# Sine of a sum in the feed-forward layer: compares and corrections replaced by two sines and column factors

## Chip, cores and metric

The kernel runs on all 8 cores of one Trainium2 chip, each core on its own batch row, without communication. The metric is the device time of the slowest core in microseconds. In the profile PE is TensorE, DVE is VectorE, ACT is ScalarE, POOL is GpSimd and SP is SyncE.

## What is computed

Two transformer layers of different make on x of shape (8, 2048, 1024): attention and a feed-forward layer, then attention and a mixture of experts, each with a residual sum and a layer norm. The change touches the first feed-forward layer:

```python
def _quantum_transform(hidden, theta, w_real, w_imag):
    imag = w_imag * jnp.sin(theta + hidden * 0.1)
    quantum_phase = jnp.cos(theta) * w_real + jnp.sin(theta) * w_imag
    return hidden + quantum_phase * imag * 0.1
hidden = jnp.einsum('bsd,df->bsf', x, W1) + b1          # 1024 -> 4096
q = _quantum_transform(hidden, quantum_phases, quantum_weights_real, quantum_weights_imag)
act = jax.nn.relu(q)
return jnp.einsum('bsf,fd->bsd', act, W2) + b2           # 4096 -> 1024
```

theta, w_real and w_imag have one value per hidden feature (4096 of them); theta is a normal value times 2 pi, so it can be well outside of -pi to pi.

## The kernel before

The activations lie transposed: a feature on each of 128 partitions, tokens along the free axis, in 8 blocks of 128 features, X in f32 and a copy XB in bf16. The 2048 tokens are cut into 4 pieces (tq) of TQ = 512.

Everything is written out by hand. The helpers vop (VectorE), aop (ScalarE) and mm (TensorE) add an instruction to their engine's program with an increment of that engine's counter (sV, sA, sT). vop and aop put a wait on the engine's own counter ahead of each instruction, so each waits until its predecessor has ended. Other waits come from the waits argument; Prog.wait leaves out one whose value the engine has already waited for. In the profile all DVE instructions stand at L323, all ACT instructions at L332, matmuls at L305 (L301 with an increment), DMA issues at L277; they are told apart by their tiles.

Prologue: constants and small vectors are loaded on SP's queue, the vectors transposed on TensorE and put into the columns of COLS. sin(theta) and cos(theta) are made once in the scratch tile PSCR (columns 320:352 and 352:384) by sin32, which reduces the argument on DVE first. COLS holds, for the feed-forward layer, theta reduced to -pi to pi (columns 32:64), ecol = 0.1 w_imag (cos(theta) w_real + sin(theta) w_imag) in 72:104 and b1 in 104:136.

ffn0 (from line 1194) treats the tokens in two halves of two pieces each. In a half, the first product runs over 8 slabs of W1 (fs), each with 4 blocks of 128 hidden features (fsub), each for both pieces (ti): 64 tiles of 128x512. A tile is 8 matmuls into one of four PSUM buffers that rotate, and then, over buffers that alternate between two places (par):

- ACT: B1 = 0.1 psum + theta (Identity, bias a column), B0 = psum (Copy), which frees the PSUM buffer
- DVE: B4 = (B1 >= pi), B1 = B1 - 2 pi B4, B4 = (B1 < -pi), B1 = B1 + 2 pi B4
- ACT: SINB = Sin(B1)
- DVE: B2 = ecol SINB + B0
- ACT: HID = Relu(B2 + b1) in bf16

The program of each engine holds the tiles one behind the other, in just this order. The second product follows in the same half: 8 blocks of output features, each for two pieces, 32 matmuls each over HID; DVE adds the result and the bias column b2 to X. W1 and W2 are loaded by POOL's queue in pieces of 1 MB into two slots of WBf, each load waiting for the last matmul that used its slot. A layer norm follows (post_ln_scoped), then attention and the experts.

Of the kernel before, what the change touches and what calls it, by code (L numbers as in the profile page):

```python
# [7 lines left out]
F32 = mybir.dt.float32  # L8
BF16 = mybir.dt.bfloat16
I32 = mybir.dt.int32  # L10
AX = mybir.AxisListType.X
AF = mybir.ActivationFunctionType
ALU = mybir.AluOpType
# [5 lines left out]
TQ = 512  # L19
# [3 lines left out]
TWO_PI = 2.0 * math.pi  # L23
# [167 lines left out]
def build_program(phases=(0, 1, 2, 3)):  # L191
# [13 lines left out]
    def sb(name, shp, dt=BF16, st=None):  # L205
        t = (st or top).enter_context(nc.sbuf_tensor(name, shp, dt))
        wb_birth[id(t)] = sT.n if "sT" in locals() or True else 0
        return t

    with top:  # L210
# [14 lines left out]
        SMALLF = sb("SMALLF", [128, 512], F32)  # L225
        COLS = sb("COLS", [128, 160], F32)
        QCOL = sb("QCOL", [128, 24], F32)
# [4 lines left out]
        CONER = sb("CONER", [1, 128], F32)  # L232
        CE64AB = sb("CE64AB", [96, 128], F32)
        CSEL128 = sb("CSEL128", [128, NC * NH], BF16)
# [12 lines left out]
        RI32A = sb("RI32A", [128, TQ], I32)  # L247
        CEPS = sb("CEPS", [128, 1], F32)

        PS = [top.enter_context(nc.psum_tensor(f"ps{i}", [128, 512], F32))  # L250
# [8 lines left out]
        def bs(pst, sem, val):  # L259
            psum_owner[id(pst)] = (sem, val)  # L260
# [56 lines left out]
        def vop(name, *args, waits=(), **kw):  # L317
            P.em("vector", lambda E, v=sV.n: E.wait_ge(sV.h, v))
            for (sem, val) in waits:
                P.wait("vector", sem, val)  # L320
            v = sV.inc()
            P.em("vector", lambda E, nm=name, a=args, k=kw:
                 getattr(E, nm)(*a, **k).then_inc(sV.h, 1))  # L323
            return v
# [47 lines left out]

        vop("memset", CEPS[:, :], EPS)
        v_x = dma("sync", "x", X[:, :].rearrange("p (c t) -> p c t", c=NC), dx.rearrange("(c p) t -> p c t", p=128))
        v_consts = 0
        for (name, tile) in (("c_ones", CONES), ("c_eye_f32", CEYEF),
                             ("c_eye_bf", CEYEB),
                             ("c_ones_row_f32", CONER), ("c_e64ab", CE64AB),
                             ("c_qsel", CSEL128),
                             ("c_tri", CTRI), ("c_iotak", CIOTAK),  # L380
                             ):
            v_consts = dma("sync", "consts", tile[0:tile.shape[0], :], dram[name])
# [4 lines left out]
        with contextlib.ExitStack() as pre:  # L387
# [70 lines left out]
            vop("tensor_scalar", COLS[:, 72:104], PSCR[:, 384:416], 0.1, None, ALU.mult)  # L458
            v_thb = v_thst

# [733 lines left out]
        def ffn0(v_in_v, a_in_a, atc_in=None):  # L1194
# [6 lines left out]
            with st:  # L1201
# [4 lines left out]
                B2 = sb("B2f", [128, 2 * TQ], F32, st)  # L1206
                B4 = sb("B4f", [128, 2 * TQ], BF16, st)
                SINB = sb("SINB", [128, 2 * TQ], F32, st)
# [7 lines left out]
                for half in range(2):  # L1216
# [3 lines left out]
                    for fs in range(8):  # L1220
# [3 lines left out]
                        for fsub in range(4):  # L1224
                            fc = fs * 4 + fsub
                            thb = COLS[:, 32 + fc:33 + fc]
                            ecol = COLS[:, 72 + fc:73 + fc]
                            b1c = COLS[:, 104 + fc:105 + fc]
                            for ti, tq in enumerate(tqs):
# [3 lines left out]
                                for c in range(NC):  # L1233
# [10 lines left out]
                                qsl = slice(par * TQ, (par + 1) * TQ)  # L1244
                                a_t = aop("activation", B1[:, qsl], pa[:, :],
                                          AF.Identity, scale=0.1, bias=thb,
                                          waits=((sT, vt), (sV, v_thb)))
                                a_t = aop("activation", B0[:, qsl], pa[:, :],
                                          AF.Copy, waits=())
                                bs(pa, sA, a_t)  # L1250
                                vop("tensor_scalar", B4[:, qsl], B1[:, qsl],
                                    math.pi, None, ALU.is_ge, waits=((sA, a_t),))
                                vop("scalar_tensor_tensor", B1[:, qsl], B4[:, qsl],
                                    -TWO_PI, B1[:, qsl], ALU.mult, ALU.add)
                                vop("tensor_scalar", B4[:, qsl], B1[:, qsl],
                                    -math.pi, None, ALU.is_lt)
                                vv = vop("scalar_tensor_tensor", B1[:, qsl],
                                         B4[:, qsl], TWO_PI, B1[:, qsl], ALU.mult,
                                         ALU.add)
                                a_sin = aop("activation", SINB[:, qsl], B1[:, qsl],  # L1260
                                            AF.Sin, waits=((sV, vv),))
                                vv = vop("scalar_tensor_tensor", B2[:, qsl],
                                         SINB[:, qsl], ecol, B0[:, qsl], ALU.mult,
                                         ALU.add,
                                         waits=((sA, a_sin),
                                                (sA, use_f.get(("rl", par), 0))))
                                dst = HID[:, fc * 1024 + ti * TQ:
# [330 lines left out]
```

## Time and profile before

| | |
|---|---|
| time, median of 2 runs | 7404.08 us (7343.23 and 7464.92) |
| profiled execution | 7338.63 us; span of its slowest core 7337.1 us |
| spans of the 8 cores | 7309.3 to 7337.1 us |
| PE busy | 4699.5 us, 64% |
| DVE busy | 2767.2 us, 38% |
| ACT busy | 2083.1 us, 28% |
| POOL busy | 170.7 us, 2% |
| DMA | 160.88 MB, mean 22 GB/s |

The profile is of one execution, on its slowest core. The span goes from the first to the last instruction; the execution's time has 1.5 us more around it. The granted clock is the share of full speed that TensorE's clock was given, as a mean over a stretch. Busy shares are means over stages of very different make; the feed-forward layer lies between 2012 and 3068 us of the span.

### The profile page before, as it was taken

To read this page: it belongs to the slowest core of one execution; us is meant where nothing else is said; L and a number is where in the kernel's file an instruction comes from. 1 tells how busy PE (TensorE), PEld (TensorE's weight loads), DVE (VectorE), ACT (ScalarE), POOL (GpSimd) and SP (SyncE) were. 2 spreads that over 40 slices of the span, in tenths; PEclk is the share of its full clock that TensorE was granted. 3 is DMA by queue.
4 is the path that set the end of the run, shared out by engine and by line. 5 is a ranking of instruction groups with operands and counts; after the bars stand their busy time and mean duration, and the time that the engine had idled before them with its cause. 6 is when DMAs were issued, how large, how long until landed. Compare 5 with 4: busy or idle time off the path is not lost.

```text
span 7337.1 us, 65020 instructions; the slowest of 8 cores (7309.3 to 7337.1 us)
## 1 busy us (share of the span) xinstructions
PE 4699.5 (64%) x17489; PEld 1732.6 (24%) x17489; DVE 2767.2 (38%) x4355; ACT 2083.1 (28%) x3175; POOL 170.7 (2%) x186
## 2 busy tenths in 40 slices
PE   1455777873255755735444667773599999998772
PEld 0221222221011311301111122221244444443230
DVE  2524422215544344346434333235433333332114
ACT  2233344533333133222122455633111111111012
POOL 0000000000000000000000000000000000000000
PEclk8777888986566866855657788886799999999885
DMA  1111000000011411400001110000222222222321
GB/s 50 24 18 12 4 9 9 1 12 0 12 18 23 52 23 18 41 12 12 0 0 15 12 12 9 1 12 0 35 35 35 35 35 35 35 35 38 55 46 46
DMA packets 236271, 160.88 MB, mean 22 GB/s; under 512 B 138921, under 2 KB 225494, under 8 KB 233878
## 3 DMA queue, kind: packets, MB, share of 16 engines
q0 software_dynamic: 232320, 138.92, 14.2%
q1 hardware_dynamic: 3606, 17.79, 0.7%
q8 instruction: 164, 2.69, 0.2%
q14 instruction: 181, 1.48, 0.1%
HBM read 287.21 MB, written 8.39 MB: 40 GB/s over the span
## 4 chain that ended last, share of the span: by engine, by line
PE 52%; DVE 25%; ACT 11%; issue 6%; DMA 5%; DVEq 1%; SPq 0%; ACTq 0%; POOL 0%; POOLq 0%
PE ps L305 36%; PE ps L301 15%; DVE SMALLF L323 6%; ACT SQR L332 3%; DVE B1f L323 2%; DVE FQR L323 2%; DVE B4f L323 2%; DVE SCpa L323 1%; DVE B2f L323 1%; DMA WBq<-w_qkv 1%; ACT HID L332 1%; ACT B1f L332 1%; DMA WBm<-ws_u 1%; DVE X L323 1%; ACT SINB L332 1%
## 5 line engine op out<-in xcount | busy, mean ns | idle before, releaser
L305 PE MATMUL ps<-XB,WBm 128*128 128x512 bf16 x4480 | 1118.5, 391 | 67.2 <-DMA WBm<-ws_g 56.3
L305 PE MATMUL ps<-PT,ARV 128*64 128x512 bf16 (+2 forms) x1152 | 485.4, 421 | 392.6 <-DVE XB L323 268.6
L305 PE MATMUL ps<-XB,WBf 128*128 128x512 bf16 x896 | 371.1, 585 | 436.5 <-ACT B0f L332 376.9
L332 ACT ACTIVATE SGR<-ps 128x512 bf16<-128x512 f32 x320 | 191.0, 597 | 1585.1 <-PE ps L301 893.2
L305 PEld LDWEIGHTS ps<-XB,WBm 128*128 128x128 bf16 x4480 | 446.3, 100 | 636.4 <-issue 139.3
L305 PE MATMUL ps<-HPAIR,WBm 128*128 128x512 bf16 x2272 | 545.7, 383 | 60.4 <-DMA WBm<-ws_d 60.4
L332 ACT ACTIVATE PT<-ps,BIASC 128x512 bf16<-128x512 f32 (+3 forms) x640 | 398.7, 623 | 492.8 <-PE ps L301 356.0
L323 DVE TENSOR_TENSOR ps<-ps,CTRI 128x128 f32<-128x128 f32 x512 | 153.5, 300 | 1015.9 <-PE ps L301 988.3
L332 ACT ACTIVATE PT<-ps,BIA 128x512 bf16<-128x512 f32 (+3 forms) x640 | 398.7, 623 | 396.8 <-PE ps L301 232.8
L301 PE MATMUL ps<-PT,CONES 128*128 128x512 bf16 (+3 forms) x1280 | 496.4, 388 | 0.0
L323 DVE RECIPROCAL SMALLF<-ps 64x512 f32<-64x512 f32 x128 | 429.4, 3355 | 66.7 <-PE ps L301 51.0
L305 PE MATMUL ps<-XB,WBkv 128*128 128x512 bf16 x960 | 323.4, 496 | 161.4 <-ACT ARK L332 86.4
L301 PE MATMUL ps<-SQR,CONES 128*128 128x512 bf16 x192 | 108.7, 566 | 409.8 <-ACT SQR L332 409.8
L323 DVE SCALAR_TENSOR_TENSOR USR<-ps,WBC 128x512 f32<-128x512 f32 x256 | 177.1, 692 | 514.4 <-PE ps L301 514.4
L323 DVE SCALAR_TENSOR_TENSOR X<-ps,X 128x512 f32<-128x512 f32 x288 | 199.2, 692 | 404.1 <-PE ps L301 402.3
L305 PEld LDWEIGHTS ps<-PT,ARV 128*64 128x64 bf16 x1152 | 126.5, 110 | 810.0 <-issue 802.5
L305 PEld LDWEIGHTS ps<-HPAIR,WBm 128*128 128x128 bf16 x2272 | 224.0, 99 | 335.8 <-issue 73.5
L305 PEld LDWEIGHTS ps<-XB,WBf 128*128 128x128 bf16 x896 | 107.6, 129 | 693.3 <-issue 677.1
L301 PE MATMUL ps<-AUXR,NEGE 128*128 128x512 bf16 x640 | 257.6, 402 | 7.5 <-DVE AUXR L323 7.5
L305 PE MATMUL ps<-ARQ,ARK 128*128 128x512 bf16 x640 | 260.9, 408 | 0.0
L301 PE MATMUL ps<-XB,WBm 128*128 128x512 bf16 x640 | 246.9, 386 | 0.0
L323 DVE TENSOR_SCALAR B4f<-B1f 128x512 bf16<-128x512 f32 x256 | 109.3, 427 | 344.6 <-ACT B0f L332 331.0
(225 smaller groups left out, 5161.7 us busy)
## 6 DMA issues: line engine op xcount, KB each, us to landing
WBf<-w_ff POOLq DMA_DIRECT2D x32, 1024.0 KB, 11.5
WBq<-w_qkv POOLq DMA_DIRECT2D x64, 256.0 KB, 4.4
WBm<-we_g POOLq DMA_DIRECT2D x16, 1024.0 KB, 11.0
WBm<-we_u POOLq DMA_DIRECT2D x16, 1024.0 KB, 15.0
WBm<-we_d POOLq DMA_DIRECT2D x16, 1024.0 KB, 11.5
X<-x SPq DMA_DIRECT2D x1, 8192.0 KB, 38.1
WBkv<-w_qkv POOLq DMA_DIRECT2D x8, 1024.0 KB, 9.2
WBm<-ws_g POOLq DMA_DIRECT2D x8, 1024.0 KB, 8.8
```

What stands on the lines that cost most here:

```text
L301: E.matmul(o, l, r, start=a, stop=b, tile_position=t)
L305: E.matmul(o, l, r, start=a, stop=b, tile_position=t))
L323: getattr(E, nm)(*a, **k).then_inc(sV.h, 1))
L332: getattr(E, nm)(*a, **k).then_inc(sA.h, 1))
```

## The change

In each tile of the first product the argument of the sine is no longer made and reduced. By sin(theta + z) = cos(theta) sin(z) + sin(theta) cos(z), with z = 0.1 psum, ACT makes B1 = Sin(z + pi/2), SINB = Sin(z) and B0 = psum, all three from PSUM and one behind the other; the third frees the PSUM buffer. DVE then makes B1 = sin(theta) B1, B1 = cos(theta) SINB + B1, and B2 = ecol B1 + B0. Relu is as before. The two compares, the two corrections and the buffer B4 go.

The prologue puts sin(theta) and cos(theta) into COLS (160:192 and 192:224) with two copies, COLS grows from 160 to 224 columns, CPI2 holds pi/2, and the constant c_e64ab, which nothing reads, is no longer loaded. The first Sin of a tile gets a wait for the B2 of the tile that used its buffers before.

```diff
--- before.py
+++ after.py
@@ -223,14 +223,13 @@
         XB = sb("XB", [128, NC * T], BF16)
         SQR = sb("SQR", [128, 2 * TQ], BF16)
         SMALLF = sb("SMALLF", [128, 512], F32)
-        COLS = sb("COLS", [128, 160], F32)
+        COLS = sb("COLS", [128, 224], F32)
         QCOL = sb("QCOL", [128, 24], F32)
         KVC = sb("KVC", [128, 8], F32)
         CONES = sb("CONES", [128, 128], BF16)
         CEYEF = sb("CEYEF", [128, 128], F32)
         CEYEB = sb("CEYEB", [128, 128], BF16)
         CONER = sb("CONER", [1, 128], F32)
-        CE64AB = sb("CE64AB", [96, 128], F32)
         CSEL128 = sb("CSEL128", [128, NC * NH], BF16)
         CTRI = sb("CTRI", [128, 128], F32)
         CIOTAK = sb("CIOTAK", [128, 16], F32)
@@ -246,6 +245,7 @@
         GSCRB = sb("GSCRB", [128, NC * 16], BF16)
         RI32A = sb("RI32A", [128, TQ], I32)
         CEPS = sb("CEPS", [128, 1], F32)
+        CPI2 = sb("CPI2", [128, 1], F32)
 
         PS = [top.enter_context(nc.psum_tensor(f"ps{i}", [128, 512], F32))
               for i in range(6)]
@@ -371,11 +371,12 @@
             slot_use[key] = max(slot_use.get(key, 0), vt)
 
         vop("memset", CEPS[:, :], EPS)
+        vop("memset", CPI2[:, :], math.pi / 2.0)
         v_x = dma("sync", "x", X[:, :].rearrange("p (c t) -> p c t", c=NC), dx.rearrange("(c p) t -> p c t", p=128))
         v_consts = 0
         for (name, tile) in (("c_ones", CONES), ("c_eye_f32", CEYEF),
                              ("c_eye_bf", CEYEB),
-                             ("c_ones_row_f32", CONER), ("c_e64ab", CE64AB),
+                             ("c_ones_row_f32", CONER),
                              ("c_qsel", CSEL128),
                              ("c_tri", CTRI), ("c_iotak", CIOTAK),
                              ):
@@ -456,7 +457,9 @@
             vop("tensor_tensor", PSCR[:, 384:416], PSCR[:, 384:416], PSCR[:, 32:64],
                 ALU.mult)
             vop("tensor_scalar", COLS[:, 72:104], PSCR[:, 384:416], 0.1, None, ALU.mult)
-            v_thb = v_thst
+            vop("tensor_copy", COLS[:, 160:192], PSCR[:, 320:352],
+                waits=((sA, va2),))
+            v_thb = vop("tensor_copy", COLS[:, 192:224], PSCR[:, 352:384])
 
             vl = dma("sync", "cols", SMALLF[0:1, 0:NH], dram["slopes"],
                      waits=((sV, sV.n), (sT, sT.n), (sA, sA.n)))
@@ -1204,7 +1207,6 @@
                 B0 = sb("B0f", [128, 2 * TQ], F32, st)
                 B1 = sb("B1f", [128, 2 * TQ], F32, st)
                 B2 = sb("B2f", [128, 2 * TQ], F32, st)
-                B4 = sb("B4f", [128, 2 * TQ], BF16, st)
                 SINB = sb("SINB", [128, 2 * TQ], F32, st)
                 w1 = dram["w_ff1"].rearrange("(c p) n -> p c n", p=128)
                 w2 = dram["w_ff2"].rearrange("(f p) n -> p f n", p=128)
@@ -1223,7 +1225,8 @@
                                      WSLOT)
                         for fsub in range(4):
                             fc = fs * 4 + fsub
-                            thb = COLS[:, 32 + fc:33 + fc]
+                            sthc = COLS[:, 160 + fc:161 + fc]
+                            cthc = COLS[:, 192 + fc:193 + fc]
                             ecol = COLS[:, 72 + fc:73 + fc]
                             b1c = COLS[:, 104 + fc:105 + fc]
                             for ti, tq in enumerate(tqs):
@@ -1242,28 +1245,26 @@
                                 wuse(WBf, slot, vt)
                                 par = (fc * 2 + ti) % 2
                                 qsl = slice(par * TQ, (par + 1) * TQ)
-                                a_t = aop("activation", B1[:, qsl], pa[:, :],
-                                          AF.Identity, scale=0.1, bias=thb,
-                                          waits=((sT, vt), (sV, v_thb)))
-                                a_t = aop("activation", B0[:, qsl], pa[:, :],
+                                a_cz = aop("activation", B1[:, qsl], pa[:, :],
+                                           AF.Sin, scale=0.1, bias=CPI2[:, 0:1],
+                                           waits=((sT, vt),
+                                                  (sV, use_f.get(("b1", par), 0))))
+                                aop("activation", SINB[:, qsl], pa[:, :],
+                                    AF.Sin, scale=0.1, waits=())
+                                a_h = aop("activation", B0[:, qsl], pa[:, :],
                                           AF.Copy, waits=())
-                                bs(pa, sA, a_t)
-                                vop("tensor_scalar", B4[:, qsl], B1[:, qsl],
-                                    math.pi, None, ALU.is_ge, waits=((sA, a_t),))
-                                vop("scalar_tensor_tensor", B1[:, qsl], B4[:, qsl],
-                                    -TWO_PI, B1[:, qsl], ALU.mult, ALU.add)
-                                vop("tensor_scalar", B4[:, qsl], B1[:, qsl],
-                                    -math.pi, None, ALU.is_lt)
-                                vv = vop("scalar_tensor_tensor", B1[:, qsl],
-                                         B4[:, qsl], TWO_PI, B1[:, qsl], ALU.mult,
-                                         ALU.add)
-                                a_sin = aop("activation", SINB[:, qsl], B1[:, qsl],
-                                            AF.Sin, waits=((sV, vv),))
+                                bs(pa, sA, a_h)
+                                vop("tensor_scalar", B1[:, qsl], B1[:, qsl],
+                                    sthc, None, ALU.mult,
+                                    waits=((sA, a_h), (sV, v_thb)))
+                                vop("scalar_tensor_tensor", B1[:, qsl],
+                                    SINB[:, qsl], cthc, B1[:, qsl], ALU.mult,
+                                    ALU.add)
                                 vv = vop("scalar_tensor_tensor", B2[:, qsl],
-                                         SINB[:, qsl], ecol, B0[:, qsl], ALU.mult,
+                                         B1[:, qsl], ecol, B0[:, qsl], ALU.mult,
                                          ALU.add,
-                                         waits=((sA, a_sin),
-                                                (sA, use_f.get(("rl", par), 0))))
+                                         waits=((sA, use_f.get(("rl", par), 0)),))
+                                use_f[("b1", par)] = vv
                                 dst = HID[:, fc * 1024 + ti * TQ:
                                           fc * 1024 + (ti + 1) * TQ]
                                 a_hid = aop("activation", dst, B2[:, qsl], AF.Relu,
```

## Rows read from the trace of the kernel before

**Rows 1.** Cores: span in us, mean granted clock.
```profile
core 0: 7309.3 us, clock 0.786
core 2: 7337.1 us, clock 0.782
```

**Rows 2.** Stretches, first half's products: length, busy (x instructions) of PE, PEld, DVE, ACT, POOL, clock, DMA.
```profile
2012.00:2439.00 427.00, 225.02 (x563) 69.36 (x564) 191.69 (x321) 169.49 (x257) 8.59 (x8) 0.63 0.16 22
2439.00:2540.00 101.00, 101.00 (x470) 45.78 (x469) 25.01 (x32) 0.38 (x1) 11.61 (x8) 1.00 0.72 73
```

**Rows 3.** Chain of waits in 2000 to 2240 us, shares by engine and line.
```profile
by line: DVE B1f L323 19.9%; DVE B4f L323 12.4%; DVE B2f L323 10.5%; ACT HID L332 10.0%; ACT B1f L332 9.8%; issue 9.8%; ACT SINB L332 9.0%; ACT B0f L332 8.6%; DMA WBf<-w_ff 5.8%; PE ps L305 1.3%; DVEq L318 0.9%; ACTq L61 0.7%; DVEq L61 0.6%
```

**Rows 4.** Timeline, ACT: start us, length us, instruction, [idle before <- released by].
```profile
2201.11 0.72 ACT L332 ACTIVATE HID<-B2f,COLS 128x512 bf16<-128x512 f32 x1 [0.96 <-DVE B2f L323]
2201.97 0.69 ACT L332 ACTIVATE B1f<-ps,COLS 128x512 f32<-128x512 f32 x1
2202.75 0.60 ACT L332 ACTIVATE B0f<-ps 128x512 f32<-128x512 f32 x1
2206.10 0.63 ACT L332 ACTIVATE SINB<-B1f 128x512 f32<-128x512 f32 x1 [2.75 <-DVE B1f L323]
2207.69 0.72 ACT L332 ACTIVATE HID<-B2f,COLS 128x512 bf16<-128x512 f32 x1 [0.96 <-DVE B2f L323]
```

**Rows 5.** Timeline, DVE, the same tile.
```profile
2203.45 0.43 DVE L323 TENSOR_SCALAR B4f<-B1f 128x512 bf16<-128x512 f32 x1 [2.44 <-ACT B0f L332]
2203.98 0.69 DVE L323 SCALAR_TENSOR_TENSOR B1f<-B4f,B1f 128x512 f32<-128x512 bf16 x1
2204.78 0.43 DVE L323 TENSOR_SCALAR B4f<-B1f 128x512 bf16<-128x512 f32 x1
2205.31 0.69 DVE L323 SCALAR_TENSOR_TENSOR B1f<-B4f,B1f 128x512 f32<-128x512 bf16 x1
2206.84 0.75 DVE L323 SCALAR_TENSOR_TENSOR B2f<-SINB,COLS,B0f 128x512 f32<-128x512 f32 x1 [0.83 <-ACT SINB L332]
```

**Rows 6.** Timeline, PE, a tile at the low clock (its 8 matmuls in two rows).
```profile
2210.07 3.14 PE L305 MATMUL ps<-XB,WBf 128*128 128x512 bf16 x7 [3.89 <-ACT B0f L332]
2213.01 0.63 PE L301 MATMUL ps<-XB,WBf 128*128 128x512 bf16 x1
```

**Rows 7.** Groups of ACT by form: count, busy us, mean ns; the last: the layer alone.
```profile
L332 ACT ACTIVATE PT<-ps,BIASC 128x512 bf16<-128x512 f32 x448 | 307.8, 687 | 397.9 <-PE ps L301 293.0 <-DVE ps L323 68.3 <-ACT PT L332 5.7
L332 ACT ACTIVATE SGR<-ps 128x512 bf16<-128x512 f32 x320 | 191.0, 597 | 1585.1 <-PE ps L301 893.2 <-DVE HPAIR L323 691.9
L332 ACT ACT_TABLE_LOAD x1 | 1.3, 1283 | 2.7 <-DVE B1f L323 2.7
```

**Rows 8.** Tile X in 2432 to 2560 us: ns min/median/max of the bias add.
```profile
L323 DVE TENSOR_SCALAR X<-X,COLS x16: 486/578/1644, 2439.6 to 2539.8; 128x512 f32<-128x512 f32 x16
```

**Rows 9.** Waits of PE in 2432 to 2545 us: total, times, longest.
```profile
PE ps L301 <- ACT HID L332: 8.9, 1, 8.9
```

**Rows 10.** Waits in 2013 to 2432 us, POOL's loads and PE's on loads.
```profile
POOL WBf L277 <- PE ps L301: 405.4, 8, 52.8
PE ps L305 <- DMA WBf<-w_ff: 59.6, 1, 59.6
```

**Rows 11.** Timeline of the prologue, SP's issues and PE's first matmul.
```profile
10.25 2.42 SPq L277 DMA_DIRECT2D CE64AB<-c_e64ab  x1
42.37 0.24 PE L314 MATMUL ps<-CEYEF,SMALLF 8*128 8x8 f32 x1 [42.37 <-DMA SMALLF<-ln_g]
```

**Rows 12.** Timeline, POOL's issues of loads and a DVE instruction beside one.
```profile
2412.68 1.67 POOL L277 DMA_DIRECT2D WBf<-w_ff  x1 [51.72 <-PE ps L301]
2442.65 1.67 POOL L277 DMA_DIRECT2D WBf<-w_ff  x1 [28.30 <-PE ps L301]
2443.06 1.49 DVE L323 TENSOR_SCALAR X<-X,COLS 128x512 f32<-128x512 f32 x1 [0.17 <-DVE X L323]
```

**Rows 13.** Timeline, DVE, bias add with no load beside it.
```profile
2439.61 0.49 DVE L323 TENSOR_SCALAR X<-X,COLS 128x512 f32<-128x512 f32 x1 [0.18 <-DVE X L323]
```

## The prediction, made before the change was run

> **What bounds the kernel now.** I read the cores first: all eight do the same work, each on its own batch row, and the slowest, core 2, has a span of 7337.1 us [rows 1]. No engine is full over the whole run, so the edited stage has to be read alone. The busy times by stretch do that [rows 2]: the first product of the feed-forward layer's first half takes some 425 us, in which PE is busy for 225 us, DVE for 192 and ACT for 169, at a granted clock of 0.63. Nobody is full. The second product of 101 us is PE at full clock from end to end. (The second half shows the same two stretches.) The chain of waits inside the first product [rows 3] says why nobody is full: DVE and ACT lines alternate (B1f, B4f, B2f, HID, SINB, B0f) and PE has 1.3%. It is a latency chain across two engines, not a throughput limit.
>
> The timelines of ACT and DVE show it tile by tile [rows 4, 5]. ACT executes in program order, and Relu of a tile (HID) waits for DVE's B2f, so the next tile's first activation stands behind it: tiles don't overlap on ACT and DVE. One period, from HID to HID, is 2201.11 to 2207.69 = 6.58 us, and 2 halves of 32 x 2 tiles make 128 periods, 842 us. PE is not the limit: at its low level (1.2 GHz) a tile runs from 2210.07 to 2213.64, 3.57 us [rows 6]; with the 0.25 us from the end of B0f to a tile's first matmul that is 3.8 us in a period of 6.58.
>
> **The period before, start to start** [rows 4, 5]: HID to B1f 0.86, B1f to B0f 0.78, B0f to the first compare 0.70, then on DVE 0.53, 0.80, 0.53, last B1f to SINB 0.79, SINB to B2f 0.74, B2f to HID 0.85. Sum 6.58, as it must be. It also gives the steps between instructions: about 0.09 us from ACT to ACT (0.15 behind HID), 0.105 from DVE to DVE, 0.10 from one engine to the other.
>
> **The period after.** Four DVE instructions go (two compares of 0.427, two corrections of 0.693). The Identity activation becomes a Sin with a pointer bias, the other Sin moves ahead and reads PSUM, and DVE gets one tensor_scalar and one scalar_tensor_tensor, each with a column pointer. Step by step:
> - HID to the first Sin: 0.86, unchanged. Its new wait is on the B2f of two tiles ago, older than what the Relu before it has waited for, so nothing is issued for it. In the first two tiles there is none.
> - First Sin, PSUM to SBUF, 128x512, bias from a column. The trace has no Sin of that form, but Exp in it takes 687 ns, and B1f 0.69 us [rows 4, 7]. To the next start 0.78.
> - Second Sin, from PSUM without pointer. Silu in that form takes 597 ns [rows 7], the old Sin from SBUF 629. I take 597, for the form decides in every other pair of rows: 0.69 to the next start (bound 0.72).
> - Copy, 597 ns as now, and the step to DVE: 0.70.
> - tensor_scalar, f32 SBUF to SBUF with one column: the form of the bias add X<-X,COLS of the second product, 486 ns undisturbed [rows 8]. With 0.105: 0.59.
> - scalar_tensor_tensor with two f32 inputs and a column: the form of B2f, 0.752 [rows 5]. With 0.105: 0.86.
> - B2f as before, to HID: 0.85. Its wait on an old Relu is again covered by a younger one.
>
> Sum 5.33; with the third decimals kept 5.32. In short: between Copy and B2f, 0.53 + 0.80 + 0.53 + 0.79 + 0.74 = 3.39 us go and 0.69 + 0.59 + 0.86 = 2.14 come. The gain is 1.26 us a tile; a misreading of 0.02 in it would be 2.5 us in all.
>
> **How many tiles count.** The second product starts under the tail of the first. The last matmul of its first group waits 8.89 us for the Relu of the tile before the last [rows 9], and its second group, which ends just before 2442.2, takes longer than the last tile's chain. So 63 of 64 tiles in each half are on the path: 126 x 1.26 = 158.8 us.
>
> **What the other parts cost.** The activation table is loaded once in the whole layer, 1.283 us [rows 7], in the first tile's chain; it moves to the front of that chain and costs the same. PSUM buffers come free after three ACT instructions instead of two, but four rotate and PE needs 3.8 of 5.32 us: nothing; without that cover it would be 0.69 a tile. The weight loads have a slot of eight tiles, 42.6 us; today PE waits for one only at the layer's start, and POOL sits up to 52.8 us before it may issue the next [rows 10]: hidden. In the prologue the SP queue issues one load less (2.42 us), but the first transposition starts at 42.37, when its column lands [rows 11], seven issues and 30 us later: no gain taken (at most 2.42). Two small copies and a memset there cost some 0.3 us each on DVE, two of them on the path: +0.6.
>
> **DVE against the issue of loads.** In the second product X<-X,COLS takes up to 1.644 us instead of 0.486 when POOL issues a weight load beside it: issue at 2442.65 for 1.67, DVE 2443.06 to 2444.55 [rows 8, 12]. The new tensor_scalar has that form, and 8 loads are issued inside each first product [rows 10]. If each met one: 16 x 1.16 = 18.5 us. By the timeline a load follows the start of the tile's last matmul by 1.2 to 1.6 us, at the low clock 4.4 to 4.8 us after the Copy; the next tensor_scalar starts at 5.42. The twelve issues of 0.87 us are about over by then, the four of 1.67 (as at 2412.68) are not. I take 2 us, bounds 0 and 18.5. The Trainium skill, "SBUF — State Buffer", section "SBUF: two separate sides", gives a rule for such rows: a DVE instruction in a two-port mode and a GpSimd one exclude each other for the whole instruction. By that rule the price per meeting is the one that the rows show, and it speaks against this form of instruction, which the first product doesn't have with f32 output today.
>
> **Sum.** The profiled execution took 7338.6 us: 7338.6 - 158.8 + 0.6 + 2 = 7182.4. I predict **7182 us**, 2.1% below it. The profiled execution lies near the lower of the two times shown (7343.2); their median, 7404, is 65 us higher, and a median over runs that spread alike would be 7247.
>
> **Rivals.**
> 1. *The steps inside an engine are wider than read.* X<-X,COLS starts 0.18 us behind the instruction that it depends on, not 0.105 [rows 13]. On the three steps that are new (Sin to Copy, and two on DVE) 0.075 more each would cost 3 x 0.075 x 126 = 28 us: 7210, within 2%. Against it: that row stands behind a second wait in its program, which none of the new ones has, and B1f behind B4f depends on its predecessor too and shows 0.105. Chance 0.13.
> 2. *DVE and POOL meet at every load*: 7338.6 - 158.2 + 18.5 = 7199. Against it stands the timing above. Chance 0.05.
> 3. *The table is reloaded.* If Sin and Copy needed different tables, one load a tile would be 128 x 1.283 = 164 us and take the gain away (7344), and two a tile would give 7508, slower. It decides from one load per tile on. Against it: one load in the layer today, with Sin, Relu, Identity and Copy mixed. Chance 0.02. The Trainium skill, "ScalarE: Activation LUTs", section "Table sets: the hidden batching unit", says that relu, copy and identity are in every set; by that rule no load is added, and the trace agrees with its one load.
> 4. *The gain is given back later.* The granted clock differs by stretch (0.63 and 1.00, [rows 2]), and shifted starts may shift where it falls and rises in the attention and expert stages. Equal cores differ by 28 us in span (7309.3 and 7337.1) [rows 1], so 10 to 20 us either way are possible: up to 7202. Chance 0.10 upward; downward it stays faster.
>
> **How the numbers follow.** The forecast has 0.70. What a measurement of this kernel can tell from no change is about 2%, here 147 us; the sum has 11 us more than that, so the wider steps, the meetings at every load and half of rival 4 end within 2%. Faster 0.76 (the forecast, and half of rival 4), within 2% 0.22, slower 0.02. The range reaches from 7150 (rival 4 downward, with the prologue's 2.42 and the 2 us of meetings saved and some rounding) to 7250 (rivals 1, 2 and 4 together, 7182 + 28 + 17 + 20 = 7247, and the median of runs that spread as before).
>
> **What would show it.** In the changed kernel HID to HID should be 5.32 us; the Sins 687 and 597 ns; the tensor_scalar 486 ns except beside a load; its successor 752; steps on DVE 0.105. The first product of each half should last some 79 us less (348 instead of 427), PE waiting there for B0f still, at a granted clock somewhat above 0.63, with one ACT_TABLE_LOAD in the layer. The second products and the other stages should keep their lengths within some 10 us. I am wrong if a Sin from PSUM takes longer than an Exp, if table loads appear, if PE becomes what ACT waits for, or if the other stages move.

## Result

| | before | changed |
|---|---|---|
| median | 7438.36 us (26 runs) | 7312.73 us (27 runs) |
| lowest | 7339.85 us | 7182.03 us |
| highest | 7662.34 us | 7496.45 us |

In most executions of either kernel some cores have a lower mean granted clock and take up to some hundred us longer, which sets the median; the ratio here and the times named below for single kernels (the lowest of each) leave such runs out. The ratio is 0.9755, with a 95% interval of 0.9707 to 0.9804: the change makes the kernel faster, and whether by more than 2% the interval just leaves open. From lowest to lowest the gain is 158 us, 2.15%. The profile after is that of the changed kernel's execution of 7180.4 us in after_again.

The cores of that execution: span and mean granted clock (they answer to [rows 1]).
```profile
core 0: 7165.9 us, clock 0.799
core 3: 7178.8 us, clock 0.798
```
Its stretches, as in [rows 2]: length, then busy time of PE, PEld, DVE, ACT and POOL with their instructions, granted clock, DMA share, GB/s. The first fence has the four products of the feed-forward layer, the second all that lies before and behind the layer.
```profile
2008.00:2353.00 345.00, 192.11 (x553) 62.13 (x552) 128.31 (x193) 167.93 (x257) 8.60 (x8) 0.74 0.19 25
2353.00:2449.00 96.00, 96.00 (x446) 43.57 (x445) 23.62 (x29) 0.00 (x0) 10.94 (x7) 1.00 0.74 77
2449.00:2798.00 349.00, 195.42 (x576) 64.07 (x575) 129.59 (x195) 166.66 (x256) 9.47 (x9) 0.76 0.20 27
2798.00:2906.00 108.00, 104.24 (x479) 46.73 (x477) 24.63 (x31) 16.84 (x11) 10.05 (x6) 0.99 0.59 59
```
```profile
0.00:2008.00 2008.00, 1129.60 (x4005) 385.10 (x4006) 702.95 (x1077) 734.39 (x1123) 37.02 (x46) 0.78 0.09 14
2906.00:4988.00 2082.00, 1122.38 (x3466) 335.66 (x3466) 855.14 (x1353) 730.87 (x1106) 39.57 (x46) 0.71 0.07 8
4988.00:6501.00 1513.00, 1399.19 (x6344) 620.01 (x6344) 605.77 (x985) 159.20 (x273) 38.23 (x46) 0.95 0.23 35
6501.00:7178.00 677.00, 396.52 (x1624) 164.23 (x1624) 167.86 (x240) 104.48 (x151) 16.80 (x18) 0.77 0.25 47
```
The same four stretches of the kernel before:
```profile
0.00:2012.00 2012.00, 1122.97 (x3997) 383.66 (x3997) 702.95 (x1074) 733.94 (x1123) 37.04 (x46) 0.78 0.09 13
3068.00:5153.00 2085.00, 1130.47 (x3466) 335.92 (x3466) 856.35 (x1354) 730.49 (x1106) 39.58 (x46) 0.70 0.07 8
5153.00:6665.00 1512.00, 1398.75 (x6344) 619.75 (x6344) 605.99 (x984) 158.95 (x273) 38.24 (x46) 0.95 0.22 35
6665.00:7337.00 672.00, 397.78 (x1624) 164.36 (x1624) 168.05 (x240) 104.54 (x151) 16.80 (x18) 0.77 0.25 47
```
The stretches end at rounded times, so the layer is better measured from its first matmul (the first row's first time) to the start of its last copy of X into XB (the second row's last time), before and after:
```profile
L305 PE MATMUL ps<-XB,WBf x896: 376/631/634, 2012.7 to 2933.1; 128*128 128x512 bf16 x180
L332 ACT ACTIVATE XB<-X x8: 1909/1910/1912, 2967.4 to 3063.3; 128x2048 bf16<-128x2048 f32 x8
```
```profile
L305 PE MATMUL ps<-XB,WBf x896: 376/586/634, 2004.7 to 2774.2; 128*128 128x512 bf16 x180
L332 ACT ACTIVATE XB<-X x8: 1910/1911/1911, 2805.2 to 2900.9; 128x2048 bf16<-128x2048 f32 x8
```
That is 1050.6 us before and 896.2 after, 154 less. Over all eight cores the layer takes 1050.6 to 1051.6 us before (mean 1051.4) and 894.7 to 896.7 after (mean 895.9), 155 less. What lies ahead of it differs from core to core by 20 us in either kernel (first matmul at 1992 to 2013 and at 1989 to 2010 us), and what lies behind it takes 4270.0 and 4270.5 us in the mean. So the difference lies in the layer. Inside, in the first half, the first product (first matmul to the start of the last Relu) fell from 426.0 to 347.4 us, and the second (from there to the first matmul of the other half) took 100.0 and 101.1. DVE's busy time in the first product fell from 192 to 128 us, while ACT, which makes one more sine from PSUM instead of a shift, stayed at 168.

A tile of the changed kernel, ACT and then DVE (start us, length us; answers to [rows 4, 5]).
```profile
2201.51 0.72 ACT L332 ACTIVATE HID<-B2f,COLS 128x512 bf16<-128x512 f32 x1 [2.40 <-DVE B2f L323]
2202.38 0.69 ACT L332 ACTIVATE B1f<-ps,CPI 128x512 f32<-128x512 f32 x1
2203.16 0.60 ACT L332 ACTIVATE SINB<-ps 128x512 f32<-128x512 f32 x1
2203.85 0.60 ACT L332 ACTIVATE B0f<-ps 128x512 f32<-128x512 f32 x1
2206.85 0.72 ACT L332 ACTIVATE HID<-B2f,COLS 128x512 bf16<-128x512 f32 x1 [2.40 <-DVE B2f L323]
```
```profile
2204.55 0.48 DVE L323 TENSOR_SCALAR B1f<-B1f,COLS 128x512 f32<-128x512 f32 x1 [3.13 <-ACT B0f L332]
2205.14 0.75 DVE L323 SCALAR_TENSOR_TENSOR B1f<-SINB,COLS,B1f 128x512 f32<-128x512 f32 x1
2206.00 0.75 DVE L323 SCALAR_TENSOR_TENSOR B2f<-B1f,COLS,B0f 128x512 f32<-128x512 f32 x1
```
HID to HID is 5.34 us. The two engines still take turns: ACT idles 2.40 us until B2f, DVE 3.13 us until B0f.

The table load, the two sines and the new DVE form over the layer (groups with count, busy us, mean ns; then by tile: ns min/median/max), and PE's wait at the start of the second product, the answer to [rows 9]:
```profile
L332 ACT ACTIVATE B1f<-ps,CPI 128x512 f32<-128x512 f32 x128 | 88.0, 688 | 121.5 <-PE ps L301 102.8 <-ACT HID L332 0.4
L332 ACT ACTIVATE SINB<-ps 128x512 f32<-128x512 f32 x128 | 76.4, 597 | 11.8
L332 ACT ACT_TABLE_LOAD x1 | 1.3, 1283 | 14.1 <-PE ps L301 14.1
...
L323 DVE TENSOR_SCALAR B1f<-B1f,COLS 128x512 f32<-128x512 f32 x128 | 62.8, 491 | 417.6 <-ACT B0f L332 417.6
```
```profile
L323 DVE TENSOR_SCALAR B1f<-B1f,COLS x128: 485/486/821, 2011.9 to 2794.8; 128x512 f32<-128x512 f32 x128
```
```profile
PE ps L301 <- ACT HID L332: 5.8, 1, 5.8
```

### The profile page after: what moved, and what is told of

The parts are those of the page before. It is cut to its first block, busy times and chain, and to the rows that moved or that the text cites. A ratio compares the mean times of both kernels' runs of the same rounds, so it can differ in the third digit from the quotient of the medians.

```text
span 7302.3 us, 63913 instructions; the slowest of 8 cores (7192.9 to 7302.3 us)
## 1 busy us (share of the span) xinstructions
PE 4729.3 (65%) x17145; PEld 1749.9 (24%) x17489; DVE 2639.7 (36%) x4102; ACT 2084.1 (29%) x3175; POOL 171.1 (2%) x186
## 4 chain that ended last, share of the span: by engine, by line
PE 53%; DVE 23%; ACT 11%; issue 6%; DMA 5%; DVEq 1%; SPq 0%; ACTq 0%; POOL 0%; POOLq 0%
PE ps L305 37%; PE ps L301 16%; DVE SMALLF L323 6%; ACT SQR L332 3%; DVE B1f L323 2%; DVE FQR L323 2%; DVE SCpa L323 1%; DMA WBq<-w_qkv 1%; DVE B2f L323 1%; ACT HID L332 1%; ACT B1f L332 1%; DMA WBm<-ws_u 1%; DVE X L323 1%; ACT SINB L332 1%; ACT B0f L332 1%
## 5 line engine op out<-in xcount | busy, mean ns | idle before, releaser
L305 PE MATMUL ps<-XB,WBm 128*128 128x512 bf16 x4375 | 1164.8, 408 | 73.1 <-DMA WBm<-ws_g 56.4
L305 PE MATMUL ps<-HPAIR,WBm 128*128 128x512 bf16 x2222 | 578.3, 404 | 63.6 <-DMA WBm<-ws_d 61.0
L305 PE MATMUL ps<-XB,WBf 128*128 128x512 bf16 x876 | 317.2, 520 | 346.8 <-ACT B0f L332 289.0
L301 PE MATMUL ps<-PT,CONES 128*128 128x512 bf16 (+3 forms) x1241 | 479.4, 386 | 0.0
L301 PE MATMUL ps<-XB,WBm 128*128 128x512 bf16 x640 | 259.0, 405 | 1.7
L305 PE MATMUL ps<-HID,WBf 128*128 128x512 bf16 x971 | 226.2, 389 | 6.6 <-ACT B0f L332 5.4
```

Source lines behind the costliest of these rows:

```text
L301: E.matmul(o, l, r, start=a, stop=b, tile_position=t)
L305: E.matmul(o, l, r, start=a, stop=b, tile_position=t))
```

## Experiments

Two theories stand against each other. The *chain theory*: a tile's ACT and DVE work is one serial chain, because Relu stands ahead of the next tile's PSUM reads in ACT's program; an instruction is worth its length and its step only where it lies in that chain. The *throughput theory*: the change saved work of DVE, and time follows the work. The kernels ran in four sets, not all on one chip; the lowest time of the kernel before was 7339.9, 7335.0, 7331.3 and 7333.8 us in them, so times of different sets compare to within some 9 us. The length of the layer, measured as above and given as a mean over the eight cores of each profile, doesn't depend on the set. Two experiments at the end ask where the spread of the times comes from.

### after_again: the changed kernel once more

> The changed kernel once more, for a profile without the lower clock level of 0.812 that the first one shows on all cores, and for more times. Chain theory (one tile's ACT and DVE work is a serial chain, 5.33 us long): a period HID to HID of 5.33 us, 63 of 64 tiles of each half count, first product about 348 us, time 7182 to 7190, ratio about 0.978. Rival (the first product became shorter but later stages pay): stages behind the layer longer than before by 10 us or more in an undisturbed execution. Second question, the median: if the change itself raised the share of disturbed executions, the medians of both kernels here lie further apart from their lowest times for the changed one; if not, they spread alike.

Lowest 7180.4 us against 7335.0 for the kernel before on the same chip. The period and the stages are shown above: 5.34 us, and what lies behind the layer takes 4270.5 us in the mean over the cores, against 4270.0 before. So nothing is given back later. The medians were 7306.1 (5 runs) and 7479.3 (7 runs), 126 and 144 us above the lowest: here the changed kernel spreads no more than the other.

### after_pipe and before_pipe: Relu behind the next tile's reads

The edit is the same in both. Relu is kept back, and issued when the next tile's PSUM reads have been:

```diff
-                                a_hid = aop("activation", dst, B2[:, qsl], AF.Relu,
-                                            bias=b1c, waits=((sV, vv),))
+                                pend_r.append((dst, B2[:, qsl], b1c, vv, par,
+                                               (fc, ti)))
...
                                 bs(pa, sA, a_h)
+                                flush_r()     # the Relu of the tile before
```

> The changed kernel with Relu of a tile put behind the three PSUM reads of the next tile in ACT's program; every instruction is kept. Chain theory: DVE's 2.3 us of a tile then run beside ACT's reads, and the period falls from 5.33 to what the fullest engine needs: ACT 0.78 + 0.69 + 0.69 + 0.86 = 3.02, or PE at its low clock, 3.42. 126 x (5.33 - 3.02 to 3.45) = 237 to 291 us less than the changed kernel: 6891 to 6945. Throughput rival (what the change saved is DVE and ACT work): same work, same time, 7182.

> The kernel before with the same move: Relu of a tile behind the next tile's Identity and Copy. Chain theory: the chain is then SINB to B1f 0.72, B1f to B0f 0.78, Copy to DVE 0.70, DVE's four instructions to SINB 2.65, together 4.85 instead of 6.58; 126 x 1.73 = 218 us less, 7121. With after_pipe it tells what the change is worth when Relu is out of the chain: 126 x (4.85 - 3.02 to 3.45) = 176 to 230 us, against 158 with Relu in it. Throughput rival: no change, 7340.

after_pipe took 6896.9 us, 283 less than the changed kernel in the same set of runs; before_pipe 7127.4, 208 less than the kernel before. The layer takes 614 instead of 896 us, and 846 instead of 1051. No instruction was removed in either, so the throughput theory falls. ACT of after_pipe:
```profile
2100.44 0.72 ACT L332 ACTIVATE HID<-B2f,COLS 128x512 bf16<-128x512 f32 x1
2101.31 0.69 ACT L332 ACTIVATE B1f<-ps,CPI 128x512 f32<-128x512 f32 x1
2102.09 0.60 ACT L332 ACTIVATE SINB<-ps 128x512 f32<-128x512 f32 x1
2102.78 0.60 ACT L332 ACTIVATE B0f<-ps 128x512 f32<-128x512 f32 x1
2103.52 0.72 ACT L332 ACTIVATE HID<-B2f,COLS 128x512 bf16<-128x512 f32 x1
```
There is no idle bracket left: ACT is full, 3.08 us a tile. In before_pipe the Sin still waits for DVE's four instructions:
```profile
2200.47 0.63 ACT L332 ACTIVATE SINB<-B1f 128x512 f32<-128x512 f32 x1 [1.88 <-DVE B1f L323]
...
2205.38 0.63 ACT L332 ACTIVATE SINB<-B1f 128x512 f32<-128x512 f32 x1 [1.88 <-DVE B1f L323]
```
The period there is 4.91, where 4.85 was expected. So the change is worth 155 us where Relu lies in the chain and 230 us where it doesn't: 1.24 us a tile (6.58 to 5.34) against 1.83 (4.91 to 3.08), because without Relu and without the Sin that waits for DVE only ACT's own work is left.

### after_fine: finer waits

```diff
-                                    waits=((sA, a_h), (sV, v_thb)))      # tensor_scalar
+                                    waits=((sA, a_cz), (sV, v_thb)))
                                 vop("scalar_tensor_tensor", B1[:, qsl],
                                     SINB[:, qsl], cthc, B1[:, qsl], ALU.mult,
-                                    ALU.add)
+                                    ALU.add, waits=((sA, a_sz),))
...
-                                         waits=((sA, use_f.get(("rl", par), 0)),))
+                                         waits=((sA, a_h), (sA, use_f.get(("rl", par), 0))))
```

> The changed kernel with finer waits: the first DVE instruction waits for the first Sin alone, the second for the second Sin, the third for the Copy. Chain theory: the Copy (0.69) and the tensor_scalar (0.59) then run beside the chain, which is HID to B1f 0.86, B1f to SINB 0.78, SINB to DVE 0.70, 0.86, 0.85 = 4.05 instead of 5.33; 126 x 1.28 = 161 us less, 7021. Throughput rival: 7182.

7033.0 us, 147 less than the changed kernel (layer 744 us, 152 less). The period is 4.13, not 4.05. DVE shows why:
```profile
2203.98 0.49 DVE L323 TENSOR_SCALAR B1f<-B1f,COLS 128x512 f32<-128x512 f32 x1 [1.76 <-ACT B1f L332]
2204.67 0.75 DVE L323 SCALAR_TENSOR_TENSOR B1f<-SINB,COLS,B1f 128x512 f32<-128x512 f32 x1 [0.20 <-ACT SINB L332]
2205.59 0.75 DVE L323 SCALAR_TENSOR_TENSOR B2f<-B1f,COLS,B0f 128x512 f32<-128x512 f32 x1 [0.17 <-DVE B1f L323]
```
B2f now has two waits to pass, and stands 0.17 us behind its predecessor instead of 0.105, although ACT's Copy had ended before that predecessor did (2205.26 against 2205.42). This is the mechanism of the first rival; it is real, and costs 0.07 us for an instruction with a second wait.

### after_plus and pipe_plus: one DVE instruction twice

In the changed kernel and in after_pipe, the last scalar_tensor_tensor is issued twice.

> The changed kernel with the last DVE instruction of a tile (B2f, 0.752 us) executed twice. Chain theory: it lies in the serial chain, 0.857 more a tile, period 6.19, 126 x 0.857 = 108 us more: 7290. Rival (DVE, busy 36% of the run, has room, so one instruction more is free): 7182.

> The same doubled DVE instruction in after_pipe, whose period is 3.09 us with ACT as its fullest engine. DVE then has 0.59 + 3 x 0.857 = 3.16 us a tile, just over ACT's 3.09. Chain theory: all but 0.07 to 0.1 of it is hidden, 10 to 15 us more than after_pipe, about 6910, where the same instruction costs 108 us in the unpipelined kernel. Rival (each DVE instruction costs its length anywhere): 108 us more, 7005.

after_plus took 7290.0 us (ratio 0.9934 to the kernel before, 0.9899 to 0.9968), 110 more than the changed kernel; pipe_plus 6923.0 (0.9427, 0.9391 to 0.9464), 26 more than after_pipe. The same instruction costs 110 us in the chain and 26 beside it; by the length of the layer, which doesn't depend on the set, 108 (1003.5 against 895.9) and 24 (637.9 against 614.3). I had expected 10 to 15 there: the step from B2f to the next tensor_scalar is 0.18 and not 0.105, so DVE needs 3.23 us a tile and has just become the fuller engine. The 0.15 us more a tile make 19 of the 24 us; the rest wasn't followed.

### relu_dve: Relu on DVE

```diff
-                                a_hid = aop("activation", dst, B2[:, qsl], AF.Relu,
-                                            bias=b1c, waits=((sV, vv),))
+                                a_hid = vop("tensor_scalar", dst, B2[:, qsl],
+                                            b1c, 0.0, ALU.add, ALU.max)
```

> The changed kernel with Relu and its bias made by DVE (tensor_scalar, add and max) instead of ACT. ACT then waits for nothing of DVE within a tile but buffers, so tiles overlap without any reordering. Chain theory: ACT 0.78 + 0.69 + 0.69 = 2.16, DVE 0.59 + 0.857 + 0.857 + 0.6 = 2.9, PE 1.73 to 3.42: period about 2.95 to 3.4, 6887 to 6940, though DVE gets more work. Rival (DVE's work sets the stage): slower than the changed kernel by 126 x 0.6 = 76 us, 7258.

6888.8 us, 292 less than the changed kernel (layer 600 us, 296 less), with one DVE instruction a tile more. ACT and then DVE:
```profile
2101.68 0.69 ACT L332 ACTIVATE B1f<-ps,CPI 128x512 f32<-128x512 f32 x1 [0.90 <-DVE B2f L323]
2102.46 0.60 ACT L332 ACTIVATE SINB<-ps 128x512 f32<-128x512 f32 x1
2103.15 0.60 ACT L332 ACTIVATE B0f<-ps 128x512 f32<-128x512 f32 x1
2104.65 0.69 ACT L332 ACTIVATE B1f<-ps,CPI 128x512 f32<-128x512 f32 x1 [0.90 <-DVE B2f L323]
```
```profile
2101.69 0.49 DVE L323 TENSOR_SCALAR HID<-B2f,COLS 128x512 bf16<-128x512 f32 x1
2102.35 0.49 DVE L323 TENSOR_SCALAR B1f<-B1f,COLS 128x512 f32<-128x512 f32 x1 [0.17 <-DVE HID L323]
2102.95 0.75 DVE L323 SCALAR_TENSOR_TENSOR B1f<-SINB,COLS,B1f 128x512 f32<-128x512 f32 x1
2103.80 0.75 DVE L323 SCALAR_TENSOR_TENSOR B2f<-B1f,COLS,B0f 128x512 f32<-128x512 f32 x1
2104.66 0.49 DVE L323 TENSOR_SCALAR HID<-B2f,COLS 128x512 bf16<-128x512 f32 x1
```
ACT waits 0.90 us for DVE to free a buffer: DVE is the full engine, at 2.97 us a tile. The throughput theory had this kernel slower than the changed one.

### pipe_nocopy: no copy of the hidden value

```diff
-                                a_h = aop("activation", B0[:, qsl], pa[:, :], AF.Copy, waits=())
-                                bs(pa, sA, a_h)
...
-                                         B1[:, qsl], ecol, B0[:, qsl], ALU.mult,
+                                         B1[:, qsl], ecol, pa[:, :], ALU.mult,
...
+                                bs(pa, sV, vv)
```

> after_pipe without the Copy to B0: the last DVE instruction reads the hidden value from PSUM, which frees its buffer later. ACT has 0.78 + 0.69 + 0.86 = 2.33 us a tile, DVE 2.3. If ACT bounds after_pipe, the period falls to about 2.4 and the time by 126 x 0.69 = 87 us, to 6810. If PE's clock or the four PSUM buffers bound it, little is gained: 6897, at most 6940 at PE's low clock of 3.42 us a tile.

6807.0 us, 90 less than after_pipe, period 2.39: 0.69 less, just the Copy and its step. So ACT was the bound in after_pipe. PE followed at a granted clock of 1.00 between 2020 and 2180 us.

### after_fold: the factor in the columns

> The changed kernel with ecol folded into the two columns in the prologue (ecol sin(theta), ecol cos(theta)): DVE makes B1 = (ecol sin(theta)) B1 + B0 and B2 = (ecol cos(theta)) SINB + B1, two scalar_tensor_tensor, and the tensor_scalar goes. Chain theory: 0.59 less in a chain of 5.33, period 4.73, 126 x 0.59 = 75 us less: 7106. It also takes away the only new DVE instruction that can meet the issue of loads. Rival (the last engine to be removed from is not in the chain, or scalar_tensor_tensor with a late operand is slower): 7182.

7101.8 us (ratio to the kernel before 0.9679, 0.9637 to 0.9721), 79 less than the changed kernel's 7180.4, period 4.73, layer 77 us less. An instruction of the chain again costs its length and its step.

### sign_best: one sine

```diff
+            vop("tensor_scalar", C1, TR, math.pi / 2.0, None, ALU.is_ge)      # prologue, TR = theta
+            vop("tensor_scalar", C2, TR, -math.pi / 2.0, None, ALU.is_lt)
+            vop("scalar_tensor_tensor", TR, C1, -math.pi, TR, ALU.mult, ALU.add)
+            vop("scalar_tensor_tensor", TR, C2, math.pi, TR, ALU.mult, ALU.add)
+            ...                                                 # ecol times 1 - 2 (C1 + C2)
...
+                                a_s = aop("activation", B1[:, qsl], pa[:, :], AF.Sin, scale=0.1,
+                                          bias=COLS[:, 32 + fc:33 + fc], ...)
+                                flush_r()
+                                vv = vop("scalar_tensor_tensor", B2[:, qsl],
+                                         B1[:, qsl], ecol, pa[:, :], ALU.mult, ALU.add, ...)
```

> Candidate. theta is brought to -pi/2 to pi/2 once in the prologue, the sign goes into ecol, so that theta + 0.1 h stays within -pi to pi and one Sin from PSUM with theta as its bias does it: B1 = Sin(0.1 psum + theta), B2 = ecol B1 + psum, HID = Relu(B2 + b1), with Relu behind the next tile's Sin. ACT 0.78 + 0.86 = 1.64 us a tile, DVE 0.93, PE 1.73 at full clock. Chain theory: PE becomes the limit, period 1.75 to 2.0 against 5.33: 126 x 3.33 to 3.58 = 420 to 451 us less than the changed kernel, 6731 to 6762. If PE falls to its low level, 3.42 us a tile: 6941.

Lowest 6747.0 us, 433 less than the changed kernel and 587 (8%) less than the kernel before in its set (7333.8). It beats both, and lies in the expected range. PE has become the bound. The profile is of a longer execution, of 6982.8 us; these rows are of core 4, whose granted clock was 0.81 between 2100 and 2200 us:
```profile
2103.43 2.01 PE L305 MATMUL ps<-XB,WBf 128*128 128x512 bf16 x7
2105.27 0.43 PE L301 MATMUL ps<-XB,WBf 128*128 128x512 bf16 x1
2105.53 2.01 PE L305 MATMUL ps<-XB,WBf 128*128 128x512 bf16 x7
```
A tile starts 2.10 us behind the last and none waits. On core 1 of the same execution, at a granted clock of 1.00, tiles start 1.73 us behind each other, also without a gap; the layer takes 446 us there and 526 on core 4. The kernel leans on 0.1 h staying small, so that theta + 0.1 h stays within -pi to pi, as the changed kernel needs it of 0.1 h + pi/2; what a larger argument would give, no run here shows.

### before_nomoe and after_nomoe: the last part left out

> The kernel before without its last part, the mixture of experts (left out with its layer norm, so its output is that of the second attention). It asks where the spread of the times comes from, by which the median of 27 runs of the changed kernel lies 131 us above their lowest and that of 26 runs before 99 us. If the spread arises in the experts' dense products, the times of this kernel agree within some 30 us; if anywhere, the spread is about two thirds of the full one. Lowest time about 7340 less 2240 us for that part: 5100.

> The changed kernel without the mixture of experts, as before_nomoe. Chain theory: 158 us less than before_nomoe, whatever the spread does: 4942. If the change raised the spread by itself, the median lies further above the lowest time here than in before_nomoe; if the spread belongs to the experts' part, both medians lie within 30 us of their lowest time.

Before: 5162.2, 5167.3, 5172.5, 5209.5 us. Changed: 5014.0, 5017.1, 5040.9, 5045.1. The medians lie 8 and 15 us above the lowest, while in the same set, on the same chip, the full kernel before ran from 7333.8 to 7691.7. Four runs of one kernel can agree by chance, as those of before_pipe do, which has the experts (7127.4 to 7147.3); that all eight agree here says that most of the spread of the time arises in the experts' part. (The 5100 expected was a slip: by the stretches that part takes 2184 us, which makes 5153.) The distance between the two is 148 us by lowest and 141 by median, with a spread of 31 to 47 us in either; the layer itself differs by 155 us in these two as well (1051.0 and 895.7).

The first profile of the changed kernel, of an execution of 7303.9 us, shows the experts' stage: core 0 and core 4, both from the end of the gate to the end of the experts' pairs.
```profile
5063.00:6486.00 1423.00, 1353.53 (x5584) 583.25 (x5699) 531.36 (x768) 144.82 (x241) 36.58 (x44) 0.90 0.20 32
```
```profile
5076.00:6412.00 1336.00, 1275.04 (x5698) 563.25 (x5699) 530.85 (x768) 144.56 (x241) 36.49 (x44) 0.97 0.21 35
```
The same work takes 87 us more at a granted clock of 0.90 than at 0.97. The lower clock isn't bound to this stage. Cores 2 and 3 of the same execution had 0.81 between 300 and 400 us, where after_again had 1.00, and came to the layer at 2062 and 2071 us, some 50 to 60 us late; behind it they needed 4268 and 4271 us, as all cores of after_again do. What makes the chip grant 0.81 in one execution and not in another was not tried.

## Why the prediction was right and wrong

**Wrong: the time and the range.** 7182 with 7150 to 7250 was forecast, and the median is 7312.73. The step that failed is the one from the single execution to the median: 7182 was worked out for an execution like the profiled one, which lay at the low end, and the upper end took the distance from it to the median, 65 us, from two runs (the 7247 of "runs that spread alike"). With 26 runs that distance is 98.5 us (7438.36 - 7339.85), in the three smaller sets of the kernel before it was 144, 28 and 233, and for the changed kernel it is 131 (27 runs) and 126 (5). 7182 plus any of these but one lies above 7250. The two runs did show that one lay 122 us above the other, so the range was too narrow by its own evidence; yet even 7182 + 122 = 7304 lies below the median that came. That the change widens the spread isn't shown: in after_again's set it was the narrower one, and the parts without the experts spread by 47 and 31 us.

**Right: the mechanism and its size.** The sum was made against an execution of 7338.6 and gave 7182.4; the lowest times are 7180.4 and 7182.0. That it came within 2 us is partly luck, for the spans of equal cores differ by 28 us, and in the two profiled cores the 158 us are made up of 154 in the layer, 8 ahead of it and -4 behind, of which only the first is shown to be the change. Point by point:
- *Chain, not throughput.* Shown by after_pipe and relu_dve (faster with all, or more, of the work) and by after_plus beside pipe_plus (one instruction, 110 us against 26).
- *The period.* 5.32 forecast, 5.34 measured. First Sin 687 against 688 ns, second 597 and 597, tensor_scalar 486 and 486, its successor 752 and 752; the steps on DVE 0.105.
- *63 of 64 tiles.* 126 x (6.58 - 5.34) = 156 us, and the layer lost 155. In the first half the first product lost 78.6 us and the second gained 1.1, where I had 79 and nothing. PE's wait for Relu fell from 8.89 to 5.8 us, without effect on the sum.
- *The table.* One load in the layer, 1283 ns, now ahead of the first Sin. No further load: the third rival is out.
- *PE.* It waits for B0f as before, and its granted clock in the first product rose from 0.63 to 0.74 and 0.76, without effect.
- *DVE beside POOL's issues.* 2 us forecast; the tensor_scalar's mean of 491 ns against its median of 486 makes 128 x 0.005 = 0.6 us. The longest is 821 ns on this core (734 to 1095 on the eight), so meetings exist, and they are few. How often they happen goes by the timing and not by how full DVE is: the longest is 1723 ns in after_pipe, and 490 in relu_dve, where DVE is fuller. The second rival is out for this kernel.
- *Steps inside an engine.* The first rival's mechanism exists (after_fine, 0.17), but the changed kernel has no instruction that issues a second wait.
- *Given back later.* Behind the layer the cores need 4270.0 us before and 4270.5 after, in the mean. The fourth rival is out in these executions.
- *Prologue.* I took no gain and 0.6 us loss. The first transposition starts at 38.3 us instead of 42.4 in the two profiled cores, but over the cores of all profiles it starts anywhere between 34.4 and 42.4 in kernels with the load and between 33.9 and 40.8 in those without it (means 38.1 and 37.1). A gain of 1 us would fit; more isn't shown. (Five issues lie between that load and the transposition, not the seven that I counted.)

The chances held 0.76 for faster by over 2%. The ratio of 0.9755 lies on that side, but its interval ends at 0.9804, so this isn't settled. Two small slips were in them: the sum has 9 us more than the 2% of 147 us (156 - 147), not 11, and 0.70 with half of rival 4 is 0.75.

## What to carry to other kernels

Where two engines are both half busy, read a period start to start on each, and look for the instruction that stands in program order ahead of the next tile's first one: moving Relu behind the next tile's reads was worth 283 us here, nearly twice the change itself, and removed no instruction. An instruction is worth its length and its step only inside the chain, so find the chain first and count its links, then cut or move them. And a forecast of a measured median needs the spread of many runs: two tell at best how far apart two can be.

## What the hardware showed that was not expected

- A granted clock of 0.81 over whole dense stretches of some executions. In the second products of sign_best's core 4 a 128x512 matmul takes 435 ns at the median, where the kernel before has 379, and in the first product eight of them take 2.10 us instead of 1.73. The experts' stage lost 87 us on one core of the first profile. In the longest run of the changed kernel (7496) four cores have a mean granted clock of 0.758 to 0.761 and the other four 0.795 to 0.800; the slowest of the latter ended 314 us before the slowest of the former.
- A second wait ahead of a DVE instruction costs 0.07 us even when it has long been met: in relu_dve the tensor_scalar B1f starts 0.17 us behind its predecessor instead of 0.105, though the Copy that it also waits for had ended 1.4 us before that predecessor.
- In after_pipe PE had gaps of over 1 us in each tile of 3.08 us and was still granted the full clock throughout (1.00 between 2020 and 2180 us), where the kernel before, with gaps of 3.2 us in the mean and up to 4.7, got 0.63.
